# A fused Mamba-2 attention and ternary FFN on one core: its hand-written order without loops, with opening and passage reordered

## The reference

```
x = layernorm(u + attn(u));  out = layernorm(x + ffn(x))

attn (Mamba-2; 8 heads of 128, state 64, chunks of 64 tokens):
  z, xBC, dt = split(u @ W_in.T)            # 1024, 1024+64+64, 8 columns
  dt  = softplus(dt + dt_bias)
  xBC = silu(conv_b + causal_conv(xBC, conv_w, width 4))   # -> x, B, C
  cum = cumsum(dt * -exp(A_log)) within a chunk
  Y   = C B^T masked by exp(cum_i - cum_j), times x*dt     # in the chunk
      + C @ carried state, times exp(cum)                  # from earlier ones
  yg  = (Y + x*D) * silu(z)
  return (yg * rsqrt(mean(yg^2)) * norm_w) @ W_out.T

ffn (expert width 2048), w_q = clip(round(w/mean|w|), -1, 1) * mean|w|:
  return (silu(x @ up_q.T) * (x @ gate_q.T)) @ down_q.T
```

## Time and profile before

| | us |
|---|---|
| median of three runs | 1370.12 (1369.99 to 1370.62) |
| the profiled execution | 1370.94 |
| its span in the trace | 1369.2 |
| PE busy in the span | 1333.5 (97%) |
| DVE busy | 1041.0 (76%) |
| ACT busy | 784.3 (57%) |
| POOL busy | 650.3 (47%) |

### The profile page before, as it was taken

How to read it: one execution, slowest core, us unless ns; L and a number is a source line. 1 busy time by engine, 2 the same in 40 slices (tenths; PEclk the granted TensorE clock), 3 DMA queues, 4 the chain that set the end, 5 groups by cost and what they waited for, 6 DMA issues and landing times.

```text
span 1369.2 us, 26933 instructions
## 1 busy us (share of the span) xinstructions
PE 1333.5 (97%) x9318; PEld 866.4 (63%) x9318; DVE 1041.0 (76%) x1857; ACT 784.3 (57%) x1561; POOL 650.3 (47%) x634
## 2 busy tenths in 40 slices
PE   7899999999999999999999999999999999999998
PEld 4455565655555646556556677777777767777774
DVE  7887887887878868788684877777777767777775
ACT  6796673874757828658474555454544545454441
POOL 0575364673755837536255534353443424353331
PEclk9899999999999999999999999999999999999999
DMA  8537334353442633424546332223122322222002
GB/s 245 167 132 228 131 110 116 89 160 101 126 127 82 174 88 99 150 86 147 142 115 214 88 118 56 72 63 85 48 62 67 74 68 56 73 62 55 32 25 69
DMA packets 162796, 143.83 MB, mean 105 GB/s; under 512 B 101344, under 2 KB 123232, under 8 KB 161504
## 3 DMA queue, kind: packets, MB, share of 16 engines
q1 hardware_dynamic: 162656, 142.05, 36.1%
HBM read 99.93 MB, written 27.39 MB: 93 GB/s over the span
## 4 chain that ended last, share of the span: by engine, by line
PE 80%; DVE 7%; issue 4%; DMA 3%; ACT 2%; POOL 2%; SPq 1%; POOLq 0%; DVEq 0%; ACTq 0%
PE ring L936 20%; PE ring L1151 15%; PE ring L965 8%; PE p_turn L1131 7%; PE p_y L1131 7%; PE p_st L1131 6%; PE p_seg L1131 5%; PE p_y L1009 3%; PE p_y L1017 2%; PE p_st L999 2%; DMA quant<-in_w_ffn 2%; PE p_turn L989 1%; DVE acc L1804 1%; PE ring L1188 1%; DVE abs_sum L1782 1%
## 5 line engine op out<-in xcount | busy, mean ns | idle before, releaser
L936 PE MATMUL ring<-u_split,weights 128*128 128x512 f16 x1620 | 375.0, 382 | 2.2 <-DVE x_ch L1809 2.0
L936 PEld LDWEIGHTS ring<-u_split,weights 128*128 128x128 f16 x1620 | 154.9, 99 | 171.9 <-issue 6.6
L1713 POOL TENSOR_TENSOR xdt<-xdt 128x512 f32<-128x512 f32 x64 | 100.6, 1571 | 340.0 <-DVE xdt L2175 340.0
L965 PE MATMUL ring<-w_out,raw 128*128 128x512 f16 x672 | 147.3, 379 | 0.2 <-issue 0.2
L1804 DVE SCALAR_TENSOR_TENSOR acc<-ring,taps,acc 128x511 f32<-128x511 f32 (+2 forms) x192 | 143.7, 749 | 4.5
L965 PEld LDWEIGHTS ring<-w_out,raw 128*128 128x128 f16 x672 | 65.7, 98 | 79.5 <-issue 0.7
L1359 ACT ACTIVATE xdt<-p_turn,dts 128x128 f32<-128x128 f32 x256 | 72.7, 375 | 70.3 <-PE p_turn L989 70.3
L1620 POOL TENSOR_TENSOR raw<-yg,raw 128x512 f16<-128x512 f32 x64 | 78.8, 1231 | 65.9 <-ACT raw L1389 65.8
L1615 POOL TENSOR_TENSOR yg<-y_ch,z_ch 128x512 f32<-128x512 f32 x64 | 81.4, 1273 | 41.4 <-DVE y_ch L1929 41.4
L1368 ACT ACTIVATE p_seg<-cum_rows,cum 128x128 f32<-128x128 f32 x256 | 80.8, 389 | 8.7 <-DVE seg L1907 8.7
L1591 POOL TENSOR_TENSOR rstd<-var_e,exponent 128x1 f32<-128x1 f32 x32 | 20.2, 631 | 118.4 <-DVE var_e L1952 118.4
(11 more groups left out here) (395 smaller groups left out, 3246.7 us busy)
## 6 DMA issues: line engine op xcount, KB each, us to landing
cum_rows<-cum_dram SPq DMA_DIRECT2D x64, 256.0 KB, 4.1
quant<-in_w_ffn SPq DMA_DIRECT2D x24, 512.0 KB, 4.4
quant<-in_w_ffn SPq DMA_DIRECT2D x48, 256.0 KB, 4.1
cum_g<-cum_dram SPq DMA_DIRECT2D x64, 128.0 KB, 4.4
rows<-in_u_tok SPq DMA_DIRECT2D x32, 256.0 KB, 4.5
x_dram<-rows SPq DMA_DIRECT2D x32, 256.0 KB, 2.1
tern_ug<-quant SPq DMA_DIRECT2D x32, 256.0 KB, 3.3
u_raw<-in_u_t SPq DMA_DIRECT2D x7, 1024.0 KB, 8.7
```

The lines of the kernel that those rows point to most:

```text
L936: mm = pe.matmul(bank_k[:, :], w_in[:, ws, k, col:col + P], us[:, par, k * T:(k + 1) * T], start=(i == 0), stop=(i == 3 * KD - 1))
L965: mm = pe.matmul(ring[b][:, :], ys[:, h, c * P:(c + 1) * P], w_out[:, ws, h, :], start=(h == 0 and ys is y_hi and ws == 0), stop=(h == H - ...
L1713: pool.tensor_tensor(tile_[:, 1, :, :], tile_[:, 0, :, :], tile_[:, 1, :, :], ALU.mult).then_inc(hid_ok, 1)
```

## The change

The loops go: `run_steps` and `ffn_steps` are now plain Python loops over all steps, every wait is on a constant, and the extra semaphore increments beside register waits are gone. The first `u` is loaded, rounded and split in four quarters, and PE's first products take them as they come. `w_lo(1)` is split in the columns of x and those of z. POOL makes the low parts of heads 2, 3 and 7, in two operations each; DVE keeps head 6, and `w_lo(5)` is gone. DVE's order in the opening and in slot (0,2) (`second_slot`) is new, the odd magnitudes have their own table (`odd_rows`), and in the passage transposes, `residual`, `chain_read` and POOL's `pow` change places.

```diff
-        def run_steps(eng, step):
-            step(0, 0)
-            step(1, 1)
-            with eng.Fori(0, QN // 2) as i:
-                step(i * 2 + Q0, 0)
-                step(i * 2 + (Q0 + 1), 1)
-            step(NB - 2, 0)
-            step(NB - 1, 1)
+        def run_steps(step):
+            for n in range(NB):
+                step(n, n % 2)
...
         def abs_rows(n, p, when):
             rows_ = {(0, 1): (None, 0, None), (0, 2): (2, None, 4), (0, 3): (None, 6, 8), (1, 0): (None, 10, 12),
                      (1, 1): (None, 14, 16, 18), (1, 2): (None, 20, 22)}
...
+        def odd_rows(n, p, when):
+            rows_ = {(0, 3): (5, 7), (1, 0): (9, 11), (1, 1): (13, 15, 17, 19), (1, 2): (21, 23)}
...
             load_raw(0)
-            sp.dma_start(u_raw[:, 0:1024], a["u_t"][0][:, 0:1024]).then_inc(u_half_in, 16)
-            sp.dma_start(u_raw[:, 1024:2048], a["u_t"][0][:, 1024:2048]).then_inc(u_in, 16)
+            for k in range(KD):
+                sp.dma_start(u_raw[:, k * T:(k + 1) * T], a["u_t"][0][:, k * T:(k + 1) * T]).then_inc(
+                    u_part_in[k] if k < KD - 1 else u_in, 16)
...
                     if p == 2:
                         if not is_at(n, 0):
                             if is_at(n, NB - 1):
-                                for j in range(4):
+                                for j in range(2):
                                     turn_x(0, 0, j)
                             store_x1(n - 1, 0)
                             load_utok(n - 1, 2)
                             if is_at(n, NB - 1):
-                                turn_x(0, 0, 4)
+                                for j in range(2, 4):
+                                    turn_x(0, 0, j)
...
                     if is_at(n, 0) and p == 2:
+                        load_wout(1)
                         load_abs(4)
                         load_abs(5)
-                        load_wout(1)
...
                     if is_at(n, 1) and p == 0:
                         load_abs(12)
+                        load_cum(n, par, 1)
                         load_abs(13)
-                        load_cum(n, par, 1)
                         load_u(2)
...
             product(0, 0, 0, 1, True)
+            pe.wait_ge(turn_free, turn_use(NB, "x01") + 1)
+            product(0, 0, 0, 5, True)
             pe.wait_ge(s1_ok, 1)
             product(0, 0, 0, 6, False)
-            pe.wait_ge(turn_free, turn_use(NB, "x01") + 1)
-            product(0, 0, 0, 5, True)
...
             chain_read(0, 0, u2, prod[6], u2_ok, c12_ok)
             gated(NB, 0, 1)
+            chain_read(0, 0, u3, prod[7], u3_ok, c21_ok)
             act.wait_ge(scales_ok, 3)
             gated(NB, 1, 0)
+            chain_read(0, 1, s1, prod[1], s1_ok, c11_ok)
             gated(NB, 1, 1)
...
+            def w_lo_head(h):
+                own, k = raw_head(h), POOL_HEADS.index(h)
+                pool.wait_ge(w_hi_ok, head_piece(h) + 1)
+                pool.tensor_scalar(own, own, SW, None, ALU.mult).then_inc(w_mul_ok, 1)
+                pool.wait_ge(w_mul_ok, k + 1)
+                pool.tensor_tensor(w_in[:, 1, :, 2 * P * h:2 * P * (h + 1)], own, w_in[:, 0, :, 2 * P * h:2 * P * (h + 1)],
+                                   ALU.subtract).then_inc(w_half_ok, 1)
...
+            w_lo_head(2)
+            w_lo_head(3)
             b_decay(0, 0, 0, turn_use(0, "b0"))
             c_decay(0, 0, 1)
             b_decay(0, 0, 1, None)
             wout_scale(0)
+            w_lo_head(7)
             wout_low(0)
...
                         if is_at(t, -1) and q == 2:
                             pool.wait_ge(ms_ok, 1)
                             pool.tensor_tensor(rms[:, :], ms[:, :], exponent[:, :], ALU.pow).then_inc(rms_ok, 1)
+                        hidden(m, k, True)
...
+            def second_slot():
+                n, par, p = 0, 0, 2
+                skip(n, p, 0)
+                skip(n, p, 1)
+                state_update(n, par, p - 1, C - 1)
+                cb_conv(1, 1, ring[ring_bank("cb", 0)])
+                dt_sum(1)
+                within(n, par, p, 0)
+                cb_silu(1, 1, ring[ring_bank("cb", 0)])
+                dt_inverse(1)
+                for c in range(C - 1):
+                    state_update(n, par, p, c)
+                within(n, par, p, 1)
+                conv(n, par, 2 * p)
+                b_read(1, 1, turn_use(0, "b"))
+                dt_third(1, 1)
+                silu(n, 2 * p)
+                z_gate(n, 2 * p)
+                cum_read(1, 1, turn_use(0, "cum"))
+                w_lo_head(6)
+                conv(n, par, 2 * p + 1)
+                silu(n, 2 * p + 1)
+                magnitude(3)
...
-                    if abs_rows(n, p, 2) is not None:
-                        magnitude(abs_rows(n, p, 2) + 1)
-                        if abs_rows(n, p, 2) == N_ABS - 2:
+                    if odd_rows(n, p, 1) is not None:
+                        magnitude(odd_rows(n, p, 1))
+                        if odd_rows(n, p, 1) == N_ABS - 1:
                             mean_magnitude()
...
                     if earlier:
                         hidden_low(*earlier, False)
+                    if attention_rest(t, q) in (0, 3):
+                        residual(NB - 1, attention_rest(t, q), p_down[attention_rest(t, q) % 2])
                     if before:
                         summed(m, k, "c12", u2, u2_ok, 5, ALU.add)
```

More of the change, by code:

```diff
@@ L68, in wait @@
 def wait(eng, sem, value):
[L70 to L80, removed]
+    if value > 0:
+        eng.wait_ge(sem, value)
 def is_at(t, value):
-    return isinstance(t, int) and t == value
+    return t == value
+POOL_HEADS = [2, 3, 7]
 def head_weights(h):
-    return 1 + h if h < 2 else 2 + h // 2
+    return 2 + h if h < 2 else 2 + h // 2
 RING = ([("x", 0), ("z", 0), ("x", 1), ("z", 1), ("x", 2), ("z", 2), ("x", 3), ("z", 3),
@@ L508, in abs_rows @@
                      (1, 1): (None, 14, 16, 18), (1, 2): (None, 20, 22)}
+            own = rows_.get((n, p), ()) if is_at(n, 0) or is_at(n, 1) else ()
+            return own[when] if when < len(own) else None
+        def odd_rows(n, p, when):
+            rows_ = {(0, 3): (5, 7), (1, 0): (9, 11), (1, 1): (13, 15, 17, 19), (1, 2): (21, 23)}
             own = rows_.get((n, p), ()) if is_at(n, 0) or is_at(n, 1) else ()
@@ L673, in turn_x @@
                 if j == 0:
-                    wait_apart(sp, prod[3], n * NQ - NQ, passed["sp"])
+                    wait(sp, prod[3], n * NQ - NQ)
                 if is_at(n, 0):
@@ L1474, in step @@
                         split_u(n + 1, 1 - par)
-                    if p == 2 and more(n):
+                    if p == 2 and more(n) and not is_at(n, 0):
                         dt_ln(n + 1)
@@ L1478, in step @@
                         magnitude(abs_rows(n, p, 1))
-                    if not end:
+                    if not end and not (is_at(n, 0) and p == 2):
                         conv_in(n, 2 * p + 1)
@@ L1551, in ffn_step @@
                         m, its, k = before
+                    if before and not (is_at(t, -1) and q == 1):
                         wait(act, act_ok, 2 * (m * NQ + k) - 1)
@@ L1827, in cb_silu, with c_silu @@
                     dve.wait_ge(cdec_ok, n * NP - NP)
+                dve.scalar_tensor_tensor(b_ch[:, :], b[N:P, :], 1.0, acc[N:P, 2, :], ALU.add,
+                                         ALU.mult).then_inc(bc_ok, 1)
+                if both:
+                    c_silu(n, par, b)
+            def c_silu(n, par, b):
                 for half in range(2):
@@ L2046, in _ @@
             dt_first(1, turn_use(0, "dt"))
+            magnitude(1)
             w_lo(4)
-            magnitude(1)
-            w_lo(5)
-            cb_conv(1, 1, ring[ring_bank("cb", 0)])
-            dt_second(1)
+            def second_slot():
[21 more added lines that the diff above has]
+                magnitude(3)
+            second_slot()
             def step(n, par):
                 first, end = is_at(n, 0), is_at(n, NB)
-                for p in range(2 if first else 0, 4):
+                for p in range(3 if first else 0, 4):
                     if gate_slot(n, p):
@@ L2065, in step @@
                         within(n, par, p, 0)
-                    if first and p == 2:
-                        cb_silu(1, 1, ring[ring_bank("cb", 0)])
-                    if abs_rows(n, p, 0) is not None:
-                        magnitude(abs_rows(n, p, 0) + 1)
                     if not end:
@@ L2143, in step @@
                         dt_second(n + 1)
+                    if odd_rows(n, p, 2) is not None:
+                        magnitude(odd_rows(n, p, 2))
                     if p == 1 and not first:
@@ L2258, in ffn_step @@
                         summed(n, q, "c11", s1, s1_ok, 2, ALU.add)
+                    if is_at(t, -1) and before:
+                        hidden(m, k, True)
                     for j in splits_at(t, q):
@@ L2268, in ffn_step @@
```

(3 more changed lines are left out.)

251 lines of the change are left out of this document (135 added, 116 removed).

## The result

The changed kernel takes 1373.98 us in the median of nine runs (1371.83 to 1376.06), the kernel before 1370.00 beside it (1369.70 to 1370.62). The ratio is 1.0027, with a 95% interval of 1.0019 to 1.0036: by the ratio 3.7 us slower (2.6 to 4.9), where 1364.6 was forecast. The profiled execution is the fastest of the nine, 1371.83 us with a span of 1369.7; the median is 2.1 above it. The single runs now lie 4.2 us apart, before 0.9, and the granted clock over the span goes from 0.994 down to 0.989; the four executions at 0.989 and 0.990 are the four longest.

What follows compares the result with a forecast made beforehand. PE (TensorE) was taken as the bound, busy 566.43 of 570 us from 110 to 680 us. Terms -2.6-7.0+7.9+1.7-5.5 = -5.5 us gave 1364.6 us as a median; 8-in-10 range 1355 to 1371.

Steps and rivals of the forecast that it cites:

- second rival: The opening gains little because ACT holds it, with low bounds for opening and passage: 1372.1 us, chance 0.12.
- signs named for the first wait: Store not before 99, load 12 near 105, PE waiting 5 to 9 us, clock about 0.6; about 3 us near 68-71.
- Loops, -2.6: Where the two loops go round, PE's issue waits of 0.98 and 1.63 us go: -2.6 us.
- Opening, -7.0: First 110 us: less DVE work ahead of skip(0,3), 5.65 us, and a new order, 1.3: -7.0, bounds -3 and -9.
- rival without a new wait: The new wait near 105 does not bite, the fifth magnitude being done early: 1355.0 us, chance 0.15.
- rival in which POOL stops DVE for all its work: In the opening POOL's 13 us of new work stop DVE outright: 1377.6 us, chance 0.08.
- The new wait, +7.9: At x_dt(1,1), load 11 waits for the later fifth odd magnitude, delaying store and cum loads: +7.9, bounds +5 and +9.5.
- Clock, +1.7: Behind the new wait, a PE tile runs at the 1.2 GHz level for most of it: +1.7 us.
- Passage, -5.5: Passage from attention to FFN: five reorderings shorten PE's waits for carry, cum_g, xdt and rows: -5.5, bounds -2 and -7.5.
- Step (e): In the passage residual(3) moves from ahead of c22 to ahead of c12: net +1.1, bounds -0.9 and +1.5.

Runs made afterwards that it cites:

- run 4: Kernel before with only both loops written out and the waits constant: 1367.51 us, ratio 0.9981 to the kernel before.
- run 11: run 8 with the quarters undone (first u in halves, w_lo(1) whole): 1360.77 us, ratio 0.9932 to the kernel before.
- run 12: run 8 with the low parts of heads 2, 3 and 7 made by DVE again: 1364.72 us, ratio 0.9963 to the kernel before.
- run 5: Changed kernel with DVE's odd magnitudes back in their old places, SP as changed: 1361.52 us, ratio 0.9942 to the kernel before.
- run 2: Changed kernel, but in block 1 SP loads u's rows ahead of load 19 of the magnitudes: 1370.75 us, ratio 1.0006 to the kernel before.
- run 8: run 3 plus products nobody reads in four of PE's remaining waits: 1361.04 us, ratio 0.9932 to the kernel before.
- run 3: Changed kernel with SP's store ahead of load 11 and its load of u's rows ahead of load 19: 1364.42 us, ratio 0.9951 to the kernel before.
- run 9: run 5 plus unread products in two PE waits (12 before cum_proj, 11 in slot (0,3)): 1362.02 us, ratio 0.9940 to the kernel before.
- run 6: Changed kernel, nothing moved, with 38 and 14 unread PE products in the waits near 105 and 160: 1371.85 us, ratio 1.0013 to the kernel before.
- run 7: run 3 with the last attention residual, residual(3), back in slot 6: 1364.97 us, ratio 0.9958 to the kernel before.
- 10: run 9 with the last attention residual, residual(3), back in slot 6: 1360.55 us, ratio 0.9931 to the kernel before.
- 13: run 8 with the last attention residual, residual(3), back in slot 6: 1359.65 us, ratio 0.9923 to the kernel before.
- run 14: Kernel before with loops written out and, of the rest of the change, only the late places of DVE's odd magnitudes: 1389.11 us, ratio 1.0133 to the kernel before.

## Why the prediction was wrong

The result, 1373.98, lies outside the range of 1355 to 1371, and above the second rival's 1372.1 too, whose cause (an opening that gains little) did not come. The signs named for the first wait all came: store at 99.44, load 12 at 105.24, PE's wait of 8.66, a clock of 0.64, a wait of 2.59 for ACT at 71. They were signs of the terms in the sum, and none of the missing one.

- **Loops, -2.6.** Right: run 4 measured -2.6, and the table has -1.1 between blocks 3 and 4.
- **Opening, -7.0.** Right in place and at first in size: -7.3 at slot (1,1). Its parts: the quarters nothing (run 11), POOL's heads 4.2 (run 12) for 4.4 in the forecast (1.20+1.20+2.04), the magnitude's place 0.9 for 1.21 (102.95 less 102.02). What is left, 2.2 for 1.3, is the new order and a clock of 1.00 to 104 us, where the kernel before has 0.95 to 110; no run parts the two. But it was taken as kept, and some of it is not. With the magnitudes where they were, 6.3 us are 4.8 at slot (1,2) (run 5): DVE's carry and seg are late next. The forecast's rival without a new wait, 1355.0, thus was some 4 us too low: the fastest execution of run 5 took 1359.1, its median 1361.5. POOL's product by a scalar took 2.78 us for a head, outside the bounds of 1.0 to 2.3 that I gave it:

```profile
18.53 2.78 POOL L1676 TENSOR_SCALAR rows<-rows 128x1024 f32<-128x1024 f32 x1 [15.69 <-ACT weights L1284]
21.40 2.13 POOL L1678 TENSOR_TENSOR weights<-rows,weights 128x1024 f16<-128x1024 f32 x1
...
47.17 3.67 POOL L1678 TENSOR_TENSOR weights<-raw,weights 128x1024 f16<-128x1024 f32 x1
```

  The three heads took 16.2 us of POOL for the 13 worked out, and POOL had the room. The rival in which POOL stops DVE for all its work fell (run 12): beside head 7's subtraction, 3.67 for 2.13, DVE's w_lo took 2.28, no more than twice a head's 1.20, so POOL was the one that waited. It was not quite free: beside POOL's first product a small operation of DVE on the chain to da took 0.96 where the kernel before has 0.19, and PE then waits 2.52 for da, before 0.8:

```profile
18.65 0.96 DVE L1910 SCALAR_TENSOR_TENSOR dts<-dt_x,dt_s 128x32 f32<-128x32 f32 x1
...
46.56 2.28 DVE L1798 SCALAR_TENSOR_TENSOR weights<-raw,weights 128x2048 f16<-128x2048 f32 x1
```

- **The new wait, +7.9.** Right: PE waited 8.66 for 0.18, on the forecast's chain, with SP's store at 99.44 (106.75 less the 7.3 gained).
- **What failed: the list of loads behind a late magnitude.** I asked "who is queued behind load 11" and named store, cum and load_u(2), and put the later odd loads at nothing, without a reason. Load 19 is the same case: it stands ahead of the load of u's rows for the block's third chunk, the fifth magnitude after it is as late, and PE waits 3.3 us at 160, with the clock low behind it. In the table slot (1,2) to (1,3) lost 6.0 us. Run 2 takes the wait away by SP's order alone, run 5 by the magnitudes' place alone.
- **Clock, +1.7.** Right for one wait in the profile (+1.2 from slot (1,1) to (1,2)), wrong as a whole. Behind the second wait it is 2.7 of the 6.0, and the median is 2.1 us above the profiled execution. I took one profile for the kernel. The single runs point to the clock: it falls by 0.004 from the shortest to the longest, an estimated 5 us of 1370, and they lie 4.2 apart. Run 8 supports it: with PE's waits filled the median is 2.6 us under run 3's, with no execution of either in the other's range. Against it stand run 9, where fills gained nothing, and the first wait, which itself was 8.66, 10.23 and 10.2 us in the profiles of the changed kernel, run 2 and run 6. How much of the 2.1 us is clock and how much a longer first wait is not shown.
- **Passage, -5.5.** Nearly right: from the start of block 7 to the end the changed kernel gains 6.6 us, of which the FFN's loop is 1.6, so -5.0. The waits for carry, rows and cum_g at 724 are gone. Step (e) was worked out at +1.1 and measured as 1.2 of waiting (run 7), and as 1.5 and 1.2 of time (runs 10 and 13), each alone within the noise; run 7 against run 3 went 0.9 the other way. DVE's rows say why, as forecast, residual(3) standing ahead of c12's sum:

```profile
794.37 0.74 DVE L1981 SCALAR_TENSOR_TENSOR rows<-ring,rms,rows 128x512 f32<-128x512 f32 x1
...
796.20 0.69 DVE L2229 TENSOR_TENSOR c_dec<-cum_g,p_turn 128x512 f32<-128x512 f32 x1
```

The sum in the profile: -7.3 (opening) +8.5 (first wait) +1.2 (clock) +6.0 (second wait and clock) -0.2 (small ones to block 3) -2.7 (loops) -5.0 (passage) = +0.5, where the forecast had -5.5. Of the 9.4 us between forecast and result the second wait is 6. Another 3 is that the median lies 2.1 above the profile, where I had put it 0.8 below; that part stays open, since only the profiled execution shows its places.

The rule of the Trainium skill that was cited on the shared port pair ("SBUF — State Buffer", SBUF: two separate sides) says that whichever of the two starts first gets the pair; the rows above agree for the two long operations, DVE's w_lo having started at 46.56 and POOL's subtraction at 47.17. They do not for the small one: POOL's product ran from 18.53 to 21.31, yet DVE's dts ended at 19.61 and da behind it took 0.19, so DVE did not stand for the whole product. POOL's spans are rough, and no run here settles it.

## What to carry to other kernels

When an operation is moved one slot later, list every instruction on the queue that waits for any one of its series, not only the first, and name for each what stands behind it: here one table of places, shifted by one, made two waits 50 us apart, and a third where W_out's load had not been moved ahead (run 14). A queue that mixes loads nobody needs soon with a store and loads on the chain should have the latter first; that was 10 us for two lines. And where a kernel is bound by PE, its short waits can have a price beyond their length, in clock, which one profile may not show: compare the single runs and their clocks before trusting it.

## What the runs showed of the hardware

The same wait of PE, 2.5 to 2.8 us near 20 us, was followed by a lower clock in some executions and not in others: the tile behind it took 2.75 us in four profiles and 4.12, 4.44 and 5.31 in three. In run 3, where waits of up to 2.8 us were left, the clock over the span was 0.994 to 0.999, with 3.7 us between the runs. With products that nobody reads in four of those waits (run 8) it was 0.999 to 1.000, with 0.7 us between them; each has five runs. On POOL a product of 128x1024 numbers by a scalar took 2.78 us, more than the subtraction of two such tensors, 2.13.
